# Two units of attention at a time within each of eight interleaved streams, and the order of all steps written anew

## What is computed

```python
x = x + tanh(g_xattn[l]) * attention_l(layernorm(x), ctx_1024)   # 16 heads of 8 features
x = x + tanh(g_ffn[l]) * feedforward_l(layernorm(x))
# attention: scores = q k^T / sqrt(8); softmax over the 256 keys; times v; times Wo, plus bo
# layer 2: causal. Layer 3: only 51 chosen rows per head keep their attention
# feed-forward: 0 top-k rows through gelu(x W); 1 two of eight experts, silu-gated, and one shared;
#   2 two of eight experts with hidden width 512 and exact gelu, and one shared; 3 fp6-quantised linear
```

## Time and profile before

| | |
|---|---|
| median of 3 runs | 1034.54 us (1033.65 to 1035.96) |
| profiled execution | 1034.86 us |
| its span, first to last instruction | 1033.0 us |
| PE busy | 913.8 us (88%) |
| DVE busy | 751.8 us (73%) |
| ACT busy | 646.0 us (63%) |
| POOL busy | 461.0 us (45%) |
| mean granted clock of TensorE | 0.956 |

### The profile page before, as it was taken

How to read it: one execution, slowest core, us unless ns; L and a number is a source line. 1 busy time by engine, 2 the same in 40 slices (tenths; PEclk the granted TensorE clock), 3 DMA queues, 4 the chain that set the end, 5 groups by cost and what they waited for, 6 DMA issues and landing times.

```text
span 1033.0 us, 22478 instructions
## 1 busy us (share of the span) xinstructions
PE 913.8 (88%) x7921; PEld 606.4 (59%) x7921; DVE 751.8 (73%) x2544; ACT 646.0 (63%) x1445; POOL 461.0 (45%) x553
## 2 busy tenths in 40 slices
PE   0379889999999999889996888999999999999873
PEld 0224345765589888357643355656469987778422
DVE  8289998776643355997798999878844356646887
ACT  0238767676686534777674666776686457786641
POOL 9822534555365203464355255555551434252332
PEclk9769999999999999999999899999999999999966
DMA  6921211101010100001112112111010010000000
GB/s 181 286 65 28 55 40 33 33 22 44 3 43 22 32 1 17 20 23 46 29 33 53 34 32 55 26 42 33 19 49 2 17 32 17 3 18 16 19 2 22
DMA packets 67037, 39.91 MB, mean 39 GB/s; under 512 B 7911, under 2 KB 64768, under 8 KB 66928
## 3 DMA queue, kind: packets, MB, share of 16 engines
q1 hardware_dynamic: 65008, 31.70, 12.0%
q0 software_dynamic: 1920, 6.78, 2.1%
HBM read 11.19 MB, written 1.05 MB: 12 GB/s over the span
## 4 chain that ended last, share of the span: by engine, by line
PE 71%; DVE 11%; POOL 7%; ACT 6%; issue 2%; DMA 1%; SPq 1%; ACTq 0%; POOLq 0%
PE A L892 12%; PE B L883 12%; PE C L738 9%; PE A L699 7%; PE A L852 6%; PE B L718 6%; DVE mx L1191 4%; PE A L685 3%; PE B L862 3%; POOL h L533 3%; ACT probs L604 3%; PE B L678 2%; PE A L823 2%; PE B L725 2%; PE A L706 2%
## 5 line engine op out<-in xcount | busy, mean ns | idle before, releaser
L1191 DVE TENSOR_REDUCE mx<-A 128x2 f32<-128x512 f32 (+1 forms) x480 | 306.9, 684 | 54.9 <-PE A L699 28.8
L604 ACT ACTIVATE probs<-B 128x512 f32<-128x512 f32 (+1 forms) x512 | 264.6, 570 | 71.2 <-PE B L718 38.2
L657 ACT ACTIVATE probs<-B,b_sb 128x256 f32<-128x256 f32 x288 | 118.9, 472 | 79.9 <-PE B L883 78.2
L529 POOL TENSOR_TENSOR rstd<-veps,mhalf 128x2 f32<-128x2 f32 x64 | 47.7, 746 | 250.2 <-DVE veps L1151 250.0
L738 PE MATMUL C<-probs,v_aug 128*9 128x256 f32 (+1 forms) x2048 | 151.2, 377 | 1.7 <-ACT probs L604 1.6
L892 PE MATMUL A<-w_sb,probs 128*128 128x128 f32 x1152 | 141.4, 277 | 0.1
L883 PE MATMUL B<-hT,w_sb 128*128 128x256 f32 x576 | 140.9, 388 | 0.1
L892 PEld LDWEIGHTS A<-w_sb,probs 128*128 128x128 f32 x1152 | 135.9, 192 | 5.7 <-issue 3.1
L699 PE MATMUL A<-k_st,q_st 64*128 64x256 bf16 (+1 forms) x1024 | 100.2, 279 | 32.8 <-DVE mx L1191 21.4
L557 POOL TENSOR_TENSOR rn<-ss,mhalf 128x32 f32<-128x32 f32 x16 | 88.0, 5501 | 90.4 <-DVE ss L1038 90.4
L883 PEld LDWEIGHTS B<-hT,w_sb 128*128 128x128 f32 x576 | 105.1, 192 | 18.7 <-issue 2.5
(11 more groups left out here) (198 smaller groups left out, 1467.1 us busy)
## 6 DMA issues: line engine op xcount, KB each, us to landing
k_st<-k_parts SPq DMA_DIRECT2D x192, 64.0 KB, 2.0
q_st<-q_parts SPq DMA_DIRECT2D x192, 64.0 KB, 2.0
w_sb<-in_w POOLq DMA_DIRECT2D x2, 2048.0 KB, 14.9
cT<-in_ctxT SPq DMA_DIRECT2D x8, 128.0 KB, 2.8
x_in<-in_x SPq DMA_DIRECT2D x8, 128.0 KB, 3.2
fc_sb<-in_fc POOLq DMA_DIRECT2D x1, 1024.0 KB, 6.3
out_x<-xs SPq DMA_DIRECT2D x8, 128.0 KB, 1.8
probs<-in_attn_w SPq DMA_DIRECT2D x1, 512.0 KB, 4.4
```

Of the source, the lines that this page charges most:

```text
L604: nc.scalar.activation(probs[s][:, part % UNIT_RING, 2 * a:2 * a + 2, 0:n], b_bank(w, a + 1)[:, 0:2 * n].rearrange("p (j q) -> p j q", j=2 ...
L657: ins = nc.scalar.activation(hid[s][:, part % UNIT_RING, c, :], b_bank(w, half + 1)[:, j * ROWS:(j + 1) * ROWS], ACT.Gelu, bias=b1_sb[:, p ...
L1191: nc.vector.tensor_reduce(mx[s][:, r, a, hp0:hp0 + n], a_bank(w, a + 1).rearrange("p (n k) -> p n k", n=n), AX.X, ALU.max).then_inc(sems[" ...
```

## The change

Within a stream the units come in twos, with both turned scores ahead of both weighings. And `TURNS_TAKEN` is another string of the same length; the counts of every stream are the same.

```diff
         units = [("attend", l, 0)]
-        for u in range(UNITS):
-            units += [("attend", l, u + 1)] * (u + 1 < UNITS) + [("weigh", l, u)]
+        units += [("attend", l, 1)]
+        for u in range(0, UNITS, UNIT_RING):
+            units += [("weigh", l, u + n) for n in range(UNIT_RING)]
+            units += [("attend", l, u + UNIT_RING + n) for n in range(UNIT_RING) if u + UNIT_RING < UNITS]
         if l == SPARSE:
             for part in range(2 * ROUNDS):
                 units.insert(2 * part + 1, ("choose", l, part))
...
 TURNS_TAKEN = """
-0000101011033112132200302000000201301213101001001001001120201200200210021121031211210312021312030011
-0131231231010122101220101000212020122003223023311030221111122311213122312220330033021033012332023330
...
-7777556756675664777777475775775664667574774775774577457757775767577567677557767757776647675457676767
-76746464767747576767676675767467675674476677
+0000101011311330222300201000300001201213010101001012010120200210020201203130121101120211320101321010
+0311321130210122002101010013220102201032033122123020121111223231211331232222310303023032031312303023
...
+7667777546767746756567466556677476676774765775766577657577567747765677757647776757676767575775465747676
+76476464767757476776767676756764775676457476
 """
```

More of the change, by code:

```diff
@@ L121 @@
 TURNS_TAKEN = """
-0000101011033112132200302000000201301213101001001001001120201200200210021121031211210312021312030011
-0131231231010122101220101000212020122003223023311030221111122311213122312220330033021033012332023330
-3320320220232123032230100003312123100130100103103100230133003230103031032011331011121120121123032220
-0120000001101102031032212321231212232012232231232323102312100010212312201102010201102101220331120212
-2101121112321122331011330330233013302123330220022202223210222103000323120130001033011303102130012131
@@ L127 @@
[L127 to L141, removed]
@@ L142 @@
-7777556756675664777777475775664667574774775774577457775757775767577567677757567776757647675456767676
-76746464767747576767675675767467675674476677
+0000101011311330222300201000300001201213010101001012010120200210020201203130121101120211320101321010
+0311321130210122002101010013220102201032033122123020121111223231211331232222310303023032031312303023
+0320203223022132032031203001231021001033101030001133210033020313021001010132330112301310211211223003
+1200000020101010102032213221322310231201122312230103323111113222010101030213310213030222212110112012
@@ new lines @@
+2123111222212213232301231031330230121333022002022222203213220103330201230213013000310113310002021213
+3101121121121201320110323310123300203121202100203222301031200222130311230100210220000133000020101121
+1000122010211330103231122221013000113032122121313212010032012021313120301310322211222113010220121212
+1002100302102200202300002022210202231213310211303002130003010010213031300103300110031001002231022323
+3023101032103311030203112101202113112331313112112221103010113311321131010302201301013220230300133330
@@ new lines @@
+3303002102221110043132414112131413112221124231413311343112243425522453425345345224223445242343232254
+2354534532445452454452524453354243423354433554432534524254244433555342354455455543354534424324554434
+2352553253233432345532325253532526656643543343456645454534543345633634363356456446334463346344466343
+6364543543365664356635346533643663446363534664343454636664653465334566646635337644547746547556444776
+4464666466474466564557575576575756755754577745745456545576467765775647457776754654577656557577545555
@@ new lines @@
+6555655555764755765654766775774566547647644467676476656766546774564476466564647475674564766744566666
+5676647666666656646675667565456756475476576575777545754545476747677467674776576465746574756454447765
+5667567565766765674557677464657754674445577644474754754777475574456677457477647757755564745655777747
+4665776645657654446575564764665447576547456477576755467564665476566564665477566447644757774476774747
+6477457464765454756546556475767474774445567445765655754775767577767574457456567767677776767577477657
@@ L144 @@
+6464674664764545645657465677765447747766456464557557647554455664556654565565566646746477777756565456
+7667777546767746756567466556677476774765775766577657577567747765677757647776757676767575775465747676
+76476464767757476776767676756764775676457476
 """
```

## The result

The changed kernel takes 1039.26 us (1038.03 to 1041.33, six runs), the one before 1034.1 us (six runs, the three of the table above among them): ratio 1.0055, interval 1.004 to 1.007. The profiled executions, from which the rows come, are 1038.23 and 1034.86 us, spans 1036.3 and 1033.0. So the rows can show 3.3 of the 5.2 us between the medians.

A forecast was written before the change was run, and what follows sets the result against it. TensorE was taken to bound the full stretches, VectorE and single chains the thin ones. Terms -3.2 + 2.4 + 0.5 - 0.3 = -0.6 us took 1034.86 to 1034.3 profiled, 1033.9 as median; range 1021 to 1047.

The forecast's parts named there:

- the even trade A: Rival, the forecast itself: merged weighings pay for the closer attends; 1033.9 us, between 1027 and 1038; chance 0.43.
- B: Rival, start and handover: ScalarE's emptying of B's banks sets the attention parts' pace; 1043.7 us, 1037 to 1049; chance 0.33.
- Term 1: TensorE: a weighing right behind a weighing saves 0.11 us; 29 new ones in the full stretches, -3.2 us.
- Term 2: Turned scores close together wait for a bank of B: +2.4 us in the full stretches (1.3 to 4.6), thin ones nothing.
- full stretches: 120 to 460 and 630 to 960 us, TensorE nearly always busy: a saved instant or added wait shows at the end.
- thin stretches: 0 to 120, 460 to 630, 960 to 1033 us (start, handover, end): VectorE and single chains set the pace.
- Term 3: Weighings soon after their own exponentials wait for them: +0.5 us (0 to 1.9) in the full stretches.
- Term 4: ScalarE's table loads in the loop fall from 42 to 38, 5.1 us less ScalarE work: -0.3 us (0 to -5.1).
- Term 5: VectorE and the ends: close maxima rise from 23 to 32, 30 in thin stretches; 0 us, bounds +3 and -3.

The follow-up runs named there:

- e3: The kernel before the change with each exponential of attention over half of its columns: 1025.5 us.
- e17: The kernel before the change with whole reduces and each exponential over 32 of 512 columns: 1024.4 us.
- e15: The kernel before the change, with the new order in steps 302 to 760, 886 to 1174, 1271 to 1318 and from 1799 on: 1030.58 us, ratio 0.9963.

## Why the prediction was wrong

I forecast 1033.9 us, no change, by the even trade A. The measured 1039.26 lies inside the range of B and of the whole (1021 to 1047), on the slower side.

- **Term 1 right.** The weighings' busy time fell by 5.2 us (4 to 5 said), and in the one full piece in which waits do not grow (302 to 760) the saving is there at the end. "An instant saved on TensorE is saved at the end" holds only so far as no new wait comes with it.
- **Term 2, a step that failed.** "Full stretches: 6 x 0.4 = +2.4": turned scores' waits rose there by 4.4 us, near my upper bound of 4.6. The price was nearly right; the count was too low. Matched with the steps, the profile after the change has 27 close attends (under 0.4 us of TensorE's work since the last one), 13 of them in the full stretches (5 and 1 before the change; the forecast had 26 and 7 for after it). Eight of the 13 wait, 4.8 us together against 0.35 before: 0.37 us for each of the 12 new ones. Six of the 13 lie within 10 us of an edge of their stretch, at 124, 129, 451, 456, 636 and 640 us. The forecast had placed the steps by their shortest lengths; that this moved close attends over an edge is likely and not shown. For the thin stretches my zero held: the waits rose there from 3.3 to 8.7 us, and TensorE's idle time did not (101.0 to 100.3). So rival B had the right kind of wait and the wrong place: its mark, waits for exponentials over 15, is met with 18.7, but the handover is 2.9 us shorter, and ScalarE's share of the chain fell. That the result lies in its range is in part luck.
- **Term 3 small, as said**: 1.6 to 2.7 us (2 to 5 said).
- **Term 4 right in count** (19, 12 and 7 loads, below), without a visible gain.
- **Term 5, the step that failed most.** "VectorE is full either way, 0": waits for reduces rose by 4.8 us in the full stretches (1.1 to 5.9), beyond my bound of 3. The reason that I gave holds for the thin stretches alone. I had placed 2 of the 32 close maxima steps in the full ones and costed none; the profile has 7 there, 2 before.
- **What to watch**: I had said that idle time in the full stretches would go from 18 to about 21; it went to 26.2. These 5 us are the miss: terms 2 and 5 together put 2.4 us where 9.2 were measured, of which idle time shows 8.1 (18.1 to 26.2) instead of about 3.

```profile
L659 ACT ACT_TABLE_LOAD x19 | 24.4, 1283 | 0.3
L606 ACT ACT_TABLE_LOAD x12 | 15.4, 1283 | 1.6 <-PE B L720 1.5
L630 ACT ACT_TABLE_LOAD x7 | 9.0, 1283 | 0.1
```

The rule that I had set against the change is that tiling speeds up the matmuls and not the emptying of PSUM (the Trainium skill, TensorEngine Tiling, section PSUM Bottleneck). This case agrees in part: over the whole kernel the loss shrinks from 5.2 to 0.6 us when the mean exponential that empties a bank goes from 570 to 368 ns. It is not the whole cause, since steps 1318 to 1799 stay 4.1 us longer with the short ones.

## What to carry to other kernels

With three banks and steps that take two, two such steps in a row can wait for the emptying of a bank: here 0.3 to 1.0 us where they waited in the full stretches, 0.4 on average over all of them, while joining two matmul groups of one shape saved 0.11. Count such places where TensorE has no slack to cover them, for every ring of banks (here reduces as well as exponentials), and don't let an edge between two stretches decide the count. A hand-written or searched order is one object with its unit list: change one and keep the other, and it costs 27 to 76 us here; a count of some waits doesn't say whether a new order is better. When an engine's work is shortened to test for a cause, compare the traces piece by piece and not only the totals: here a level total hid a gain of 2.8 us and a loss of 4.1. Where two orders have issued the same steps, the faster pieces can be joined.

## What was not expected of the hardware

- **An exponential's time has a large fixed part.** The 570 and 368 ns above are means over two shapes. By shape, 128x512 takes 597 ns (the kernel before), 128x256 382 and 128x128 275 (e3), and 128x32 195 (e17). From the first two an estimate is 0.84 ns a column and 167 ns whatever the length; it gives 194 ns for 32 columns. The rows of the kernel before and of e17:

```profile
L604 ACT ACTIVATE probs<-B 128x512 f32<-128x512 f32 x448 | 243.5, 597 | 62.3 <-PE B L718 38.2 <-PE B L725 18.2
...
L604 ACT ACTIVATE probs<-B 128x32 f32<-128x32 f32 x512 | 73.4, 195 | 148.1 <-PE B L718 105.1
```

- **The clock at the start differed between two profiles, at a cost of 0.6 us.** In the first 120 us e15 and the kernel before issue the same steps. The granted clock was 1.00 in one and 0.86 in the other, where it was at the lower of its two levels (1.2 GHz) from 48 to 72 us and in two shorter stretches before. What TensorE did ahead of that was the same in both: busy 3.6 us of every 10 from 30 to 50 us. In e15:

```profile
0.00:120.00 120.00, 67.99 (x593) 33.63 (x597) 91.35 (x255) 50.23 (x107) 70.36 (x106) 1.00 0.46 128
```

Step 302 came at 165.9 and at 166.5 us. From 50 to 60 us, at the lower level, TensorE waited 0.84 to 0.87 us for reduces before each maxima step, so that slower matmuls cost little there:

```profile
51.20 0.61 PE L699 MATMUL A<-k_st,q_st 64*128 64x256 bf16 x4 [0.87 <-DVE mx L1191]
```
